# Order of a turn and of the feed-forward jobs in a six-layer attention stack on one core

## The chip, the cores and the metric

One core of a Trainium2 chip runs the whole program. The metric is device time in microseconds of one execution; the median of three runs of the kernel before is 1388.38 us (1385.80 to 1391.52). The engines are TensorE (PE, matrix products), VectorE (DVE), ScalarE (ACT), GpSimd (POOL) and SyncE (SP), which issues the transfers. Each works through its own list in order, and they meet only at semaphores. Banks are the eight PSUM banks of 128 x 512 fp32.

## The reference

Three blocks follow each other on x of 2 x 512 x 128, each with a residual and a layer norm: a Mamba block with a mixture of experts, a cross attention, and a stack of six layers. The change touches only the stack:

```python
def local_attention(q, k, v):      # windows of 32, each sees itself and the one before
    ...
    sim = jnp.einsum('bhwie,bhwje->bhwij', bq, bk2) * QK_SCALE
    sim = jnp.where(mask, -jnp.finfo(sim.dtype).max, sim)
    attn = jax.nn.softmax(sim, -1)
    out = jnp.einsum('bhwij,bhwje->bhwie', attn, bv2)
def attn_layer(x, Wqkv, qs, ksc, Wo):
    ...                            # 16 heads of 64: q, k = l2norm * scale, then rotary with a scale
def ffn_layer(x, g, bln, W1, b1, W2, b2):
    mu = x.mean(-1, keepdims=True)
    var = ((x - mu) ** 2).mean(-1, keepdims=True)
    xn = (x - mu) / jnp.sqrt(var + 1e-05) * g + bln
    hg = xn @ W1 + b1
    a, gate = jnp.split(hg, 2, -1)
    return a * jax.nn.gelu(gate, approximate=False) @ W2 + b2
for i in range(DEPTH):             # DEPTH = 6
    x = attn_layer(shift_tokens(x), ...) + x
    x = ffn_layer(shift_tokens(x), ...) + x
```

The hidden width of the feed-forward is 341, so gates and values come in groups of 128, 128 and 85 rows.

## The kernel before

The stack (`build_stack`) is a software pipeline of turns, 16 to a layer. Channels lie on the partitions and the 512 positions of a batch entry on the free axis. A layer has 16 units, eight for each of two batch entries; a unit h is q (even h) or k (odd h) of four heads on the side of projection and rotation, and a unit n is two heads on the side of scores, softmax and values. The first and the last layer stand alone; the four layers between run in a loop (`all_turns`, lines 1175 to 1180), so the first has four turns of filling before it and the last four turns of draining behind it.

In turn t the engines work on several units at once:

- PE (`body`, line 1370): scores of unit t+1 (line 1299 adds the mask, 1305 the products), projection of unit t+4 into two banks (1266 to 1270), transposes of the probabilities of unit t (1317), output projection of t-1 (1339), values' projection of t+1 (1290), head norm of t+4 (1278), values of t (1329).
- ACT (`body`, 1462): copy of the output of t-1 (1437), square of the projected pair (1413), exponential of the scores of t+1 (1481), copies of the transposed probabilities (1444) and of v (1453), logarithm and root for the head norm (1420, 1424).
- DVE (`body`, 1587): normalisation of unit t+3 (1543), in some turns a cast of the next layer's weights (1523), maximum (1603) and subtraction (1609) of t+1, the two rotary products of t+4 (1532, 1533), row sum (1626) and reciprocal (1630) of t+1.
- POOL (`body`, 1650): probabilities of unit t times the reciprocal (1657), sum of the two squares of t+4 (1666), the two sums of the rotary products of t+4 (1668, 1669), in some turns the low part of the next layer's weights (1648).
- SP (`body`, 1215): places the normalised heads of t+3 by transfers, four for q (1203) and eight for k (1207), then shifts v of t+1 (1212, 1213), then weights.

The two banks of the projected pair exist once: the projection of the next unit waits for both products of this one. The scores of an even unit need the k unit normalised one turn earlier. In turns 7 to 14 of all layers but the last, DVE and POOL also split the next layer's weights into a high and a low part (`high_weights`, `low_weights`), and in turns 11 and 12 ACT scales the rotary table (`scale_table`, 1431).

The feed-forward of a batch entry is a job of four stages, one in each of four turns (`Steps.stage`, 1169): t modulo 8 is 0 to 3. Job 0 of a layer lies in its turns 8 to 11, job 1 in turns 0 to 3 of the next layer. Stage 0: residual (1551), mean (1343), centring (1567), square (1501). Stage 1: variance at the head of PE's turn (1347), its root on ACT (1471, 1473), scale and shift (1574, 1576), gate 0 (1356) and value 0 (1363), gelu 0 (1459) and gate 1. Stage 2: gelu 1, value 1, gate 2, gelu 2, value 2. Stage 3: down projection (1368), second residual (1558), and the new stream split into a high part by ACT (1505) and a low part by DVE (1635), for which the projection of the first unit of that batch entry in the next layer waits. Gates are put into the job's output bank, values into the bank of v, so gates and values alternate one by one; each gelu has a table load before it and another behind it (1460), which brings back the table of logarithm and exponential.

Of the kernel before, what the change touches and what calls it, by code (L numbers as in the profile page):

```python
# [11 lines left out]
ALU = mybir.AluOpType  # L12
# [1073 lines left out]
def build_stack(nc, ctx, Y, places, spare, d, C):  # L1086
# [164 lines left out]
    def _(pe):  # L1251
# [28 lines left out]
        def project_v(s, n, before):  # L1280
# [4 lines left out]
            if before[1] in (1, 2):  # L1285
                pe.wait_ge(*act_done.at(s.turn, 3 * before[0] + (1 if before[1] == 1 else 3)))
# [62 lines left out]
        def up_gate(s, job, j):  # L1349

            if j == 0:
                pe.wait_ge(*ffn_in.at(s.turn, 80 * (job + 1) if job < 1 else 80))
                pe.wait_ge(*centre_step.at(s.turn, 3 * job + 3))
            else:
                pe.wait_ge(*gate_done.at(s.turn, 3 * job + j))
            mm(OUT_BANK[job % 2][0:ROWS[j], :], w1[:, HID + P * j:HID + P * j + ROWS[j]], xn[:], start=True, stop=True).then_inc(up_done.sem, 1)

        def up_value(s, t, job, j):

            pe.wait_ge(*v_copied.at(s.turn, min(t + 2, UNITS) if s.last else t + 2))  # L1360
            if act_done.any(s.turn, 3 * job + j):
                pe.wait_ge(*act_done.at(s.turn, 3 * job + j))
            mm(V_BANK[0:ROWS[j], :], w1[:, P * j:P * j + ROWS[j]], xn[:], start=True, stop=True).then_inc(up_done.sem, 1)
# [6 lines left out]
        def body(s):  # L1370
            for t in s.range:
                (job, stage), before = s.stage(t), s.stage(t - 1)
# [33 lines left out]
    def _(ac):  # L1406
# [48 lines left out]
        def gelu(s, job, j):  # L1455
            ac.wait_ge(*up_done.at(s.turn, 6 * job + (1, 3, 4)[j]))
            if act_done.any(s.turn, 3 * job + j // 2):
                ac.wait_ge(*act_done.at(s.turn, 3 * job + j // 2))
            A(gate[0:ROWS[j], j % 2, :], OUT_BANK[job % 2][0:ROWS[j], :], ACT.Gelu, bias=ffn_param[0:ROWS[j], 5 + j:6 + j]).then_inc(gate_done.sem, 1)
            nc.scalar.preload_act_table_set("natural_log_exp_and_others")  # L1460

        def body(s):
            for t in s.range:
                job, stage = s.stage(t)
                if t >= 0 and s.unit(t - 1):
                    copy_out(s, t - 1)
# [7 lines left out]
                if stage == 2:  # L1474
                    gelu(s, job, 1)
# [10 lines left out]
                if stage == 1:  # L1486
                    ac.wait_ge(*ffn_in.at(s.turn, 80 * (job + 1) if job < 1 else 80))
                    gelu(s, job, 0)
                if stage == 2:
                    gelu(s, job, 2)  # L1490
                if t in (11, 12) and not s.last:
                    ac.wait_ge(*product_done.at(s.turn, 2 * (t + 4)))
                    scale_table(s, t - 11, 1)
                if s.unit(t + 4):
                    logarithm(s, t + 4)
                    root(s, t + 4)
                if stage == 0:
# [3 lines left out]
                    A(dsq[:], dx[:], ACT.Square).then_inc(rstd_step.sem, 1)  # L1501
                if s.resplit(job, stage):
# [14 lines left out]
    def _(dv):  # L1517
# [60 lines left out]
        def gated(s, job, j):  # L1578
            rows = ROWS[j]
            dv.wait_ge(*gate_done.at(s.turn, 3 * job + j + 1))  # L1580
            dv.wait_ge(*up_done.at(s.turn, 6 * job + (2, 5, 6)[j]))
# [321 lines left out]
```

## Time and profile before

| | us |
|---|---|
| median of 3 runs | 1388.38 |
| the profiled execution, its own time | 1386.02 |
| its span | 1383.9 |
| PE busy | 1169.6 (85%) |
| DVE busy | 981.7 (71%) |
| ACT busy | 866.7 (63%) |
| POOL busy | 677.9 (49%) |

All times in the rows are microseconds from the start of the span. The stack runs from about 380 to 1371; a layer is about 155 to 161 us. Busy shares are those of the whole span, in which the stack is 70%; the order inside one turn has to be read from the timelines. The lines of the helper functions are those of the kernel before, and tiles of earlier blocks reused by the stack carry their old names (h is the squares, x the sine products, mo_w the cosine products or the normalised probabilities).

### The profile page before, as it was taken

To read this page: it belongs to the slowest core of one execution; us is meant where nothing else is said; L and a number is where in the kernel's file an instruction comes from. 1 tells how busy PE (TensorE), PEld (TensorE's weight loads), DVE (VectorE), ACT (ScalarE), POOL (GpSimd) and SP (SyncE) were. 2 spreads that over 40 slices of the span, in tenths; PEclk is the share of its full clock that TensorE was granted. 3 is DMA by queue.
4 is the path that set the end of the run, shared out by engine and by line. 5 is a ranking of instruction groups with operands and counts; after the bars stand their busy time and mean duration, and the time that the engine had idled before them with its cause. 6 is when DMAs were issued, how large, how long until landed. Compare 5 with 4: busy or idle time off the path is not lost. (4 is left out here: it accounts for less than half of the span.)

```text
span 1383.9 us, 27095 instructions
## 1 busy us (share of the span) xinstructions
PE 1169.6 (85%) x9636; PEld 720.0 (52%) x9636; DVE 981.7 (71%) x1207; ACT 866.7 (63%) x1284; POOL 677.9 (49%) x522
## 2 busy tenths in 40 slices
PE   7787789997658988998978988898988989899875
PEld 3222257774225555565555655565555555556541
DVE  2798867775647777867776787677876777777743
ACT  5553366664345677676867667586866758686744
POOL 1555434442246555646564565546564465645420
PEclk9899979999869999999999999999999999999997
DMA  3000053102013533434333433334333442434220
GB/s 104 1 0 0 1 129 122 55 1 70 23 31 91 144 76 86 110 101 104 77 99 83 127 82 86 101 87 122 78 91 86 113 106 71 103 84 113 68 60 15
DMA packets 75528, 107.32 MB, mean 78 GB/s; under 512 B 25347, under 2 KB 31938, under 8 KB 75002
## 3 DMA queue, kind: packets, MB, share of 16 engines
q1 hardware_dynamic: 75386, 105.47, 29.1%
q8 instruction: 84, 1.38, 0.4%
q14 instruction: 58, 0.48, 0.1%
HBM read 30.89 MB, written 0.59 MB: 23 GB/s over the span
## 5 line engine op out<-in xcount | busy, mean ns | idle before, releaser
L1543 DVE SCALAR_TENSOR_TENSOR st_turned<-st_rn,mo_w 128x1024 f32<-128x1024 f32 x96 | 154.9, 1613 | 150.6 <-POOL mo_w L1669 94.1
L1666 POOL TENSOR_TENSOR st_sq_sum<-h 128x512 f32<-128x512 f32 x96 | 126.6, 1318 | 220.6 <-ACT h L1413 220.6
L1668 POOL TENSOR_TENSOR mo_w<-mo_w,x 128x512 f32<-128x512 f32 x96 | 122.3, 1274 | 185.0 <-DVE mo_w L1533 185.0
L1413 ACT ACTIVATE h<-banks 128x1024 f32<-128x1024 f32 x96 | 98.3, 1024 | 145.8 <-PE banks L1270 145.7
L1532 DVE TENSOR_TENSOR x<-banks,st_scaled 128x1024 f32<-128x1024 f32 x96 | 116.8, 1217 | 26.2 <-ACT h L1413 25.9
L1329 PEld LDWEIGHTS banks<-st_p_blocks,st_vs 128*64 128x64 f32 x1536 | 83.0, 140 | 97.3 <-issue 96.0
L1278 PE MATMUL banks<-st_sq_sum,head_ones 128*128 128x512 f32 x192 | 105.8, 633 | 31.4 <-POOL st_sq_sum L1666 29.9
L1657 POOL TENSOR_TENSOR mo_w<-st_prob,st_ri 128x512 f32<-128x512 f32 x96 | 123.8, 1289 | 15.1 <-DVE st_ri L1630 14.5
L1290 PEld LDWEIGHTS banks<-st_wv,stream 128*128 128x128 f32 x768 | 100.7, 191 | 45.1 <-issue 45.0
L1329 PE MATMUL banks<-st_p_blocks,st_vs 128*64 128x64 f32 x1536 | 101.9, 231 | 25.1 <-ACT st_p_blocks L1444 24.9
L1669 POOL TENSOR_TENSOR mo_w<-mo_w,x 128x512 f32<-128x512 f32 x96 | 122.5, 1276 | 0.0
L1533 DVE TENSOR_TENSOR mo_w<-banks,st_scaled 128x1024 f32<-128x1024 f32 x96 | 116.5, 1214 | 0.0
L1444 ACT ACTIVATE st_p_blocks<-banks 64x512 f32<-64x512 f32 x192 | 112.1, 584 | 3.2 <-PE banks L1317 0.8
L430 POOL TENSOR_TENSOR ma_dbx<-ma_u,ma_b_rows 128x1024 f32<-128x1024 f32 x32 | 75.4, 2359 | 74.6 <-ACT ma_b_rows L288 51.6
L1481 ACT ACTIVATE st_prob<-st_prob 128x512 f32<-128x512 f32 x96 | 60.4, 629 | 77.4 <-DVE st_prob L1609 77.1
L1305 PE MATMUL banks<-st_k_blocks,st_qT 128*32 128x128 f32 x3072 | 108.7, 284 | 0.0
L1266 PE MATMUL banks<-st_y_high,st_w_high 128*128 128x512 f32 x192 | 90.6, 472 | 15.9 <-POOL st_w_low L1648 8.6
L1290 PE MATMUL banks<-st_wv,stream 128*128 128x128 f32 x768 | 101.2, 275 | 0.0
L1305 PEld LDWEIGHTS banks<-st_k_blocks,st_qT 128*32 128x32 f32 x3072 | 81.4, 113 | 37.6 <-issue 37.1
L1339 PE MATMUL banks<-x,st_wo 128*128 128x512 f32 x192 | 98.4, 594 | 0.8 <-ACT x L1437 0.8
L1329 PE MATMUL banks<-st_p_blocks,st_vn 128*64 128x64 f32 x1536 | 98.3, 225 | 0.0
L370 DVE TENSOR_TENSOR_SCAN ma_state<-banks,ma_dbx 128x512 f32<-128x512 f32 x64 | 76.0, 1213 | 13.5 <-ACT banks L298 11.0
(229 smaller groups left out, 2680.7 us busy)
## 6 DMA issues: line engine op xcount, KB each, us to landing
st_qT<-st_turned SPq DMA_DIRECT2D x192, 128.0 KB, 2.3
st_k_blocks<-st_turned SPq DMA_DIRECT2D x384, 64.0 KB, 2.0
st_vs<-st_vn SPq DMA_DIRECT2D x96, 192.0 KB, 2.5
st_w_raw<-in_w_qk SPq DMA_DIRECT2D x12, 512.0 KB, 5.3
st_vs<-st_vn SPq DMA_DIRECT2D x96, 48.0 KB, 2.1
mo_w_all<-gate_rows SPq DMA_DIRECT2D x1, 3072.0 KB, 13.0
st_wv<-in_w_v SPq DMA_DIRECT2D x12, 256.0 KB, 2.9
st_wo<-in_wo SPq DMA_DIRECT2D x12, 256.0 KB, 3.7
```

What stands on the lines that cost most here:

```text
L1278: mm(NORM_BANK, C["head_ones"], sq_sum[:], start=True, stop=True).then_inc(norm_done.sem, 1)
L1290: last = mm(V_BANK[:, rows], Y[:, b, rows], wv[:, pair, :], start=True, stop=True)
L1305: last = mm(SCORE_BANK[rows].rearrange("p (o h i k) -> p o h i k", o=2, h=2, i=2)[:, odd, :, i, :], qT[:, r, pair, t0:t0 + WIN], k_blocks[ ...
L1329: last = mm(TURN_BANK[rows, P * j:P * j + P].rearrange("p (h o q) -> p h o q", h=2, q=WIN)[:, :, odd, :], (vn if odd else vs)[:, r, j, row ...
L1444: A(p_blocks[rows, r, half, :], TURN_BANK[rows, :], ACT.Copy).then_inc(pt_copied.sem, 1)
L1532: v.tensor_tensor(sin_part[:], QK_BANKS, scaled[:, which, 1], ALU.mult).then_inc(product_done.sem, 1)
L1533: v.tensor_tensor(cos_part[:, which], QK_BANKS, scaled[:, which, 0], ALU.mult).then_inc(product_done.sem, 1)
L1543: v.scalar_tensor_tensor(turned[:, h % 4], rn[:, h % 2, :].unsqueeze(1).to_broadcast([P, 2, SEQ]), 1e12, cos_part[:, which], ALU.min, ALU. ...
L1657: nc.gpsimd.tensor_tensor(pn[:, r], prob[:, r], ri[:, r, :].unsqueeze(2).to_broadcast([P, 8, 64]), ALU.mult).then_inc(pn_done.sem, 1)
L1666: nc.gpsimd.tensor_tensor(sq_sum[:], sq[:, 0, :], sq[:, 1, :], ALU.add).then_inc(sq_summed.sem, 1)
L1668: nc.gpsimd.tensor_tensor(cos_part[:, which, 0, :], cos_part[:, which, 0, :], sin_part[:, 1, :], ALU.subtract).then_inc(add_done.sem, 1)
L1669: nc.gpsimd.tensor_tensor(cos_part[:, which, 1, :], cos_part[:, which, 1, :], sin_part[:, 0, :], ALU.add).then_inc(add_done.sem, 1)
```

## The change

No matrix product is added or taken away in number, and no transfer. The order of instructions on four engines changes, and what waits for what with it.

- DVE: in a turn the maximum and the difference come first, then normalisation, cast, and the feed-forward's residual, scaling or gating, then row sum and reciprocal; the rotary products come behind them, then centring or second residual.
- POOL: the sum of squares comes first, then the probabilities of unit t+1 (no longer of unit t, one turn later), then the two rotary sums.
- ACT: the copy of the output of unit t comes at the end of turn t, behind logarithm and root, no longer at the head of turn t+1; the gelus come behind it. Gelus 0 and 1 stand together in stage 1 with one restore of the table behind the pair. The scaling of the rotary table comes behind the copy of the output.
- PE: gate 1 goes to the bank of v at the end of stage 1, value 0 and value 1 come early in stage 2, value 2 early in stage 3, and the down projection in the same stage 3 behind the head norm. The output and values' projections keep their place before the head norm.

```diff
@@ PE, body
+                if stage == 2:
+                    up_value(s, t, job, 0)
+                    up_value(s, t, job, 1)
+                if stage == 3:
+                    up_value(s, t, job, 2)
                 if s.unit(t) and t >= 0:
                     turn_probs(s, t)
-                if stage == 3:
-                    down(s, job)
                 if t >= 0 and s.unit(t - 1):
                     out_proj(s, t - 1)
                 if t >= -1 and s.unit(t + 1):
-                    project_v(s, t + 1, before)
+                    project_v(s, t + 1, job, stage)
+                if s.unit(t + 4):
+                    head_norm(s, t + 4)
                 if stage == 0:
                     mean(s, job)
                 if stage in (1, 2):
-                    up_gate(s, job, 0 if stage == 1 else 2)
-                if s.unit(t + 4):
-                    head_norm(s, t + 4)
-                if stage in (1, 2):
-                    up_value(s, t, job, stage - 1)
+                    up_gate(s, t, job, 0 if stage == 1 else 2)
+                if stage == 3:
+                    down(s, job)
                 if s.unit(t) and t >= 0:
                     values(s, t)
                 if stage == 1:
-                    up_gate(s, job, 1)
-                if stage == 2:
-                    up_value(s, t, job, 2)
+                    up_gate(s, t, job, 1)
@@ ACT, gelu and body
-            ac.wait_ge(*up_done.at(s.turn, 6 * job + (1, 3, 4)[j]))
+            ac.wait_ge(*up_done.at(s.turn, 6 * job + (1, 2, 5)[j]))
-            A(gate[0:ROWS[j], j % 2, :], OUT_BANK[job % 2][0:ROWS[j], :], ACT.Gelu, ...)
-            nc.scalar.preload_act_table_set("natural_log_exp_and_others")
+            A(gate[0:ROWS[j], j % 2, :], (V_BANK if j == 1 else OUT_BANK[job % 2])[0:ROWS[j], :], ACT.Gelu, ...)
-                if t >= 0 and s.unit(t - 1):
-                    copy_out(s, t - 1)
...
-                if stage == 2:
-                    gelu(s, job, 1)
...
                 if s.unit(t + 4):
                     logarithm(s, t + 4)
                     root(s, t + 4)
+                if t >= 0 and s.unit(t):
+                    copy_out(s, t)
...
+                if stage == 1:
+                    ac.wait_ge(*ffn_in.at(s.turn, 80 * (job + 1) if job < 1 else 80))
+                    gelu(s, job, 0)
+                    gelu(s, job, 1)
+                    nc.scalar.preload_act_table_set("natural_log_exp_and_others")
+                if stage == 2:
+                    gelu(s, job, 2)
+                    nc.scalar.preload_act_table_set("natural_log_exp_and_others")
+                if t in (11, 12) and not s.last:
+                    ac.wait_ge(*product_done.at(s.turn, 2 * (t + 4)))
+                    scale_table(s, t - 11, 1)
@@ DVE, body: maximum and difference now stand ahead of this
+                if t >= -3 and s.unit(t + 3):
+                    normalise_heads(s, t + 3)
+                ...                                    # casts, as before
                 if stage == 0:
                     residual1(s, job)
                 if stage == 1:
                     scale_centred(s, job)
-                if s.unit(t + 4):
-                    rotate(s, t + 4)
-                if stage == 0:
-                    centre(s, job)
+                if stage == 2:
+                    gated(s, job, 0)
+                    gated(s, job, 1)
                 if stage == 3:
-                    residual2(s, job)
-                if stage == 2:
-                    gated(s, job, 1)
+                    gated(s, job, 2)
                 ...                                    # row sum and reciprocal of t + 1, as before
-                if stage in (1, 2):
-                    gated(s, job, 0 if stage == 1 else 2)
+                if s.unit(t + 4):
+                    rotate(s, t + 4)
+                if stage == 0:
+                    centre(s, job)
+                if stage == 3:
+                    residual2(s, job)
@@ POOL, body
-                ...                                    # probabilities of t, low weights, sum of squares, rotary sums
+                ...                                    # low weights, sum of squares
+                n = t + 1
+                if s.unit(n) and n >= 0:
+                    r = n % 2
+                    pool.wait_ge(*rec_done.at(s.turn, n + 1))
+                    if t_done.any(s.turn, n - 1):
+                        pool.wait_ge(*t_done.at(s.turn, n - 1))
+                    nc.gpsimd.tensor_tensor(pn[:, r], prob[:, r], ri[:, r, :]..., ALU.mult).then_inc(pn_done.sem, 1)
+                ...                                    # rotary sums of t + 4
```

## Rows read from the trace of the kernel before

**Rows 1.** The page's group of line 1543 (busy, mean ns, idle before, releaser).

```profile
L1543 DVE SCALAR_TENSOR_TENSOR st_turned<-st_rn,mo_w 128x1024 f32<-128x1024 f32 x96 | 154.9, 1613 | 150.6 <-POOL mo_w L1669 94.1
```

**Rows 2.** Timeline of DVE, one plain turn (start, us, engine, line, what, idle before).

```profile
781.37 0.68 DVE L1603 TENSOR_REDUCE st_mx<-banks 128x8 f32<-128x512 f32 x1
...
783.82 1.21 DVE L1533 TENSOR_TENSOR mo_w<-banks,st_scaled 128x1024 f32<-128x1024 f32 x1
...
785.66 0.20 DVE L1630 RECIPROCAL st_ri<-st_rs 128x8 f32<-128x8 f32 x1
787.65 2.05 DVE L1543 SCALAR_TENSOR_TENSOR st_turned<-st_rn,mo_w 128x1024 f32<-128x1024 f32 x1 [1.79 <-POOL mo_w L1669]
789.63 0.68 DVE L1603 TENSOR_REDUCE st_mx<-banks 128x8 f32<-128x512 f32 x1
```

**Rows 3.** Timeline of POOL, the same turn.

```profile
785.11 1.27 POOL L1668 TENSOR_TENSOR mo_w<-mo_w,x 128x512 f32<-128x512 f32 x1 [1.72 <-DVE mo_w L1533]
...
787.58 1.04 POOL L1657 TENSOR_TENSOR mo_w<-st_prob,st_ri 128x512 f32<-128x512 f32 x1
789.88 1.27 POOL L1666 TENSOR_TENSOR st_sq_sum<-h 128x512 f32<-128x512 f32 x1 [1.26 <-ACT h L1413]
```

**Rows 4.** Timeline of DVE, a normalisation with POOL idle.

```profile
750.50 1.22 DVE L1543 SCALAR_TENSOR_TENSOR st_turned<-st_rn,mo_w 128x1024 f32<-128x1024 f32 x1 [1.89 <-ACT st_rn L1424]
```

**Rows 5.** Timeline of PE, a stage 3 turn in which it never waits.

```profile
760.59 0.38 PE L1299 MATMUL banks<-mask,ident 128*128 128x512 bf16 x1
...
761.90 0.50 PE L1266 MATMUL banks<-st_y_high,st_w_high 128*128 128x512 f32 x1
...
763.84 2.74 PE L1368 MATMUL banks<-st_act,st_w 128*128 128x512 f32 x6
766.42 1.02 PE L1339 MATMUL banks<-x,st_wo 128*128 128x512 f32 x2
...
768.17 1.02 PE L1278 MATMUL banks<-st_sq_sum,head_ones 128*128 128x512 f32 x2
...
770.21 0.39 PE L1299 MATMUL banks<-mask,ident 128*128 128x512 bf16 x1
```

**Rows 6.** Timeline of ACT, the square of the same turn.

```profile
763.60 1.02 ACT L1413 ACTIVATE h<-banks 128x1024 f32<-128x1024 f32 x1 [0.89 <-PE banks L1270]
```

**Rows 7.** Timelines of SP and PE, where scores wait for k.

```profile
790.38 4.99 SPq L1207 DMA_DIRECT2D st_k_blocks<-st_turned  x8
...
794.27 0.39 PE L1299 MATMUL banks<-mask,ident 128*128 128x512 bf16 x1 [0.18 <-DMA st_k_blocks<-st_turned]
```

**Rows 8.** Source view of line 1523, ns min/median/max.

```profile
L1523 DVE CAST st_w_high<-st_w_raw x48: 280/708/1356, 388.3 to 1190.2; 128x256 fp32r<-128x256 f32 x48
```

**Rows 9.** Timeline of DVE, maxima of turns 0, 4, 8, 12, 15 of layer 1.

```profile
571.24 0.68 DVE L1603 TENSOR_REDUCE st_mx<-banks 128x8 f32<-128x512 f32 x1
...
612.87 0.69 DVE L1603 TENSOR_REDUCE st_mx<-banks 128x8 f32<-128x512 f32 x1
...
646.87 0.68 DVE L1603 TENSOR_REDUCE st_mx<-banks 128x8 f32<-128x512 f32 x1
...
690.72 0.69 DVE L1603 TENSOR_REDUCE st_mx<-banks 128x8 f32<-128x512 f32 x1
...
717.93 0.68 DVE L1603 TENSOR_REDUCE st_mx<-banks 128x8 f32<-128x512 f32 x1
```

**Rows 10.** Timelines of DVE and ACT, a stage 0.

```profile
1208.88 1.41 DVE L1551 TENSOR_TENSOR stream<-banks,stream 64x512 f32<-64x512 f32 x2
...
1213.72 0.61 ACT L1501 ACTIVATE st_dsq<-st_dx 128x512 f32<-128x512 f32 x1
```

**Rows 11.** Timeline of ACT, a table load in the drain.

```profile
1356.67 1.28 ACT L1459 ACT_TABLE_LOAD   x1 [3.62 <-PE banks L1356]
```

**Rows 12.** Timeline of PE and windows (us, engines' busy time, PEclk, DMA).

```profile
1185.61 0.48 PE L1329 MATMUL banks<-st_p_blocks,st_vs 128*64 128x64 f32 x4 [2.20 <-ACT st_p_blocks L1444]
...
1185.00:1188.50 3.50, 2.89 (x44) 2.34 (x47) 1.76 (x3) 2.96 (x5) 2.46 (x3) 0.57 0.24 70
```

More of the change, by code:

```diff
@@ L1278, in head_norm, with project_v @@
             mm(NORM_BANK, C["head_ones"], sq_sum[:], start=True, stop=True).then_inc(norm_done.sem, 1)
-        def project_v(s, n, before):
+        def project_v(s, n, job, stage):
             b, pair = n // 8 % 2, n % 8
@@ L1284, in project_v @@
                 pe.wait_ge(*v_copied.at(s.turn, n))
-            if before[1] in (1, 2):
-                pe.wait_ge(*act_done.at(s.turn, 3 * before[0] + (1 if before[1] == 1 else 3)))
+            if stage in (2, 3):
+                pe.wait_ge(*act_done.at(s.turn, 3 * job + stage))
             pe.wait_ge(*wv_in[pair // 4].at(s.turn, 16 * (n // 16) + 16))
@@ L1353, in up_gate, with up_value @@
                 pe.wait_ge(*centre_step.at(s.turn, 3 * job + 3))
-            else:
[L1355 to L1363, printed above, removed]
+            if j == 1:
+                pe.wait_ge(*v_copied.at(s.turn, min(t + 2, UNITS) if s.last else t + 2))
+            if j == 2:
+                pe.wait_ge(*act_done.at(s.turn, 3 * job + 1))
+            bank = V_BANK if j == 1 else OUT_BANK[job % 2]
+            mm(bank[0:ROWS[j], :], w1[:, HID + P * j:HID + P * j + ROWS[j]], xn[:], start=True, stop=True).then_inc(up_done.sem, 1)
+        def up_value(s, t, job, j):
+            if j < 2:
+                pe.wait_ge(*gate_done.at(s.turn, 3 * job + j + 1))
+            else:
+                pe.wait_ge(*v_copied.at(s.turn, min(t + 1, UNITS) if s.last else t + 1))
+                pe.wait_ge(*act_done.at(s.turn, 3 * job + 2))
+            bank = OUT_BANK[job % 2] if j == 0 else V_BANK
+            mm(bank[0:ROWS[j], :], w1[:, P * j:P * j + ROWS[j]], xn[:], start=True, stop=True).then_inc(up_done.sem, 1)
         def down(s, job):
@@ L1371, in body @@
             for t in s.range:
-                (job, stage), before = s.stage(t), s.stage(t - 1)
+                job, stage = s.stage(t)
                 if stage == 1:
@@ L1485, in body @@
                     copy_v(s, t + 1)
-                if stage == 1:
-                    ac.wait_ge(*ffn_in.at(s.turn, 80 * (job + 1) if job < 1 else 80))
-                    gelu(s, job, 0)
-                if stage == 2:
[L1490 to L1493, printed above, removed]
                 if s.unit(t + 4):
@@ L1589, in body @@
                 job, stage = s.stage(t)
-                if t >= -3 and s.unit(t + 3):
-                    normalise_heads(s, t + 3)
-                if s.first and t + 5 < PARTS:
-                    high_weights(s, t + 5, 0)
-                if t >= PARTS - 1 and t < 2 * PARTS - 1 and not s.last:
-                    high_weights(s, t - PARTS + 1, 1)
                 n = t + 1
@@ L1609, in body @@
                     v.tensor_tensor(prob[:, r], bank, mx[:, r, :].unsqueeze(2).to_broadcast([P, 8, 64]), ALU.subtract).then_inc(sub_done.sem, 1)
+                if t >= -3 and s.unit(t + 3):
+                    normalise_heads(s, t + 3)
+                if s.first and t + 5 < PARTS:
+                    high_weights(s, t + 5, 0)
+                if t >= PARTS - 1 and t < 2 * PARTS - 1 and not s.last:
+                    high_weights(s, t - PARTS + 1, 1)
                 if stage == 0:
@@ L1651, in body @@
             for t in s.range:
[L1652 to L1657 removed]
                 if s.first and t + 5 < PARTS:
                     low_weights(s, t + 5, 0)
[L1660 to L1662 removed]
+                h = t + 4
+                if s.unit(h):
                     pool.wait_ge(*sq_done.at(s.turn, h + 1))
```

21 lines of the change are left out of this document (7 added, 14 removed).

## The prediction

> **What bounds the kernel now.** I read the page's groups first. The stack's own groups occur 96 times each, one per turn, and the costliest VectorE group, the normalisation in line 1543, stands idle before its start for 150.6 us, 94.1 us of it for GpSimd's second sum (line 1669) [rows 1]. Then the timelines, engine by engine, over one undisturbed turn of the third layer. VectorE begins the maximum at 781.37 and the next one at 789.63: a turn is 8.26 us [rows 2]. The loop that sets this: the second product (line 1533) ends at 785.03; GpSimd starts the first sum 0.08 later and both take 2.47 up to the start of line 1657 [rows 2, 3]; the normalisation starts 0.07 after that (787.65), takes 2.05 and the maximum follows at once (789.63); from a maximum to the start of the second product are 2.45 (783.82 - 781.37), and that product takes 1.21 [rows 2]. 0.08 + 2.47 + 0.07 + 1.98 + 2.45 + 1.21 = 8.26, the whole turn. VectorE idles 1.79 in it. The normalisation's 2.05 is itself a price of the order: GpSimd's line 1657 runs beside it from 787.58 [rows 3], and where nothing runs beside it the same instruction takes 1.22 [rows 4].
>
> PE is the engine behind. A feed-forward turn in which it never waits shows all its steps: scores 1.31 (760.59 to 761.90), projection with transposes 1.94 (to 763.84), down projection 2.58 (to 766.42), output and value projections 1.75 (to 768.17), head norm and values 2.04 (to 770.21) [rows 5]. Without the down projection a turn costs PE 7.04. So a plain turn can lose at most 1.2 of its 8.26.
>
> **Plain turn, after.** Zero is the start of PE's scores. Projection starts at 1.31; ACT's square starts 1.70 after it (763.60 against 761.90) and takes 1.02 [rows 5, 6], so it ends at 4.03. GpSimd's sum of squares, now first on its queue, starts 0.08 later and takes 1.27 [rows 3]: 5.38. PE has by then done transposes, output and value projection (1.31 + 1.94 + 1.75 = 5.00) and waits 0.44 for it; head norm and values end at 5.44 + 2.04 = 7.48. On VectorE the maximum starts at 1.44, the subtraction ends at 2.84; the normalisation waits for the sums. They began after the products of the turn before, which end at 7.84: the exponential (square's end less the overlap, 3.93 + 0.63 = 4.56) releases the row sum; from a product's end to the reciprocal's start are 0.63, its length 0.20 (785.66) [rows 2], so reciprocal ends at 5.5, products at 7.84, sums at 7.92 + 2.47 = 10.4, which is 2.95 in a turn of 7.48. Normalisation alone then: 2.98 to 4.21, before the sum of squares starts at 4.11. Its old neighbour, line 1657, now runs beside the products. So VectorE and GpSimd no longer bound; 7.48 is PE's, with head norm's wait in it.
>
> But what is late next is the key transfer. After each odd unit SP issues eight transfers of k; the next scores need the first four. In the one place where PE is seen waiting for them, the first issue is at 790.38 and scores start at 794.27: 3.89 later [rows 7]. Before, normalisation ended at 789.70 and its late first issue left just enough. Now it ends at 4.21, so every second turn's scores come at 4.21 + 0.02 + 3.89 = 8.12 instead of 7.48. Mean of the pair: 7.80, against 8.26: a gain of 0.46 per plain turn. The shifts of v, queued on SP behind the eight issues (4.99 long), go out at 9.2 instead of on time; values wants them some 5 later, so that costs nothing.
>
> The eight turns a layer that also cast weights (line 1523) add 0.28 to 1.36, median 0.71 [rows 8]; it ran mostly beside line 1657 in its long form. Now it falls beside the sum of squares, so I take 1.1, nearer the long end. (The Trainium skill, GPSIMD Engine Reference, section Key points, says GpSimd contends with VectorE instructions of two SBUF inputs or in a two-port mode, the normalisation and the cast here; the 2.05 against 1.22 agrees. If the cast ran alone, some 0.8 per casting turn outside the feed-forward would go, 4 turns a layer.)
>
> **Feed-forward jobs.** Turn starts of layer 1 (the second) in VectorE's timeline give what they cost now [rows 9]: a job without casts 612.87 - 571.24 = 41.6; four turns after it 34.0; a job with casts 43.85; the next three 27.2 (with the fourth, as a plain turn of 8.3, 35.5).
> Stage 0, after: the residual (1.41 [rows 10]) now stands between normalisation and row sum; it also waits for the output projection, 3.25 + 1.02 + 0.04 = 4.31 [rows 5], so it ends at 5.72; row sum, reciprocal and products follow to 9.02; centring, of the maximum's size (0.68), 9.62; ACT's square 0.61 [rows 10], 10.27; variance, at the head of PE's next turn, from 10.3, one product of head norm's form, about 1.0, next scores 11.3. PE has been ready since 8.3 (7.48 and the mean's product). That is worse than now by 1.5, and it opens a gap of 2.0 on PE.
> Stage 1: scale and shift, two VectorE instructions of at most 0.7, end by 5.6, and gate 0 is wanted at 6.3; PE runs through with two more products of the output projection's form, half of that 1.75 each: 7.48 + 1.75 = 9.2. Stage 2: ACT does both gelus after one table load. A load is 1.28 [rows 11]; a gelu I take at 0.7, a little over the square of its size, 0.61 [rows 10]. Copy of the output ends at 9.0, so gelus end at 10.95 and 11.65, the restore at 12.9: in stage 2, 1.75, 2.4 and 3.7. Value 0 is wanted at 2.81: hidden. The square starts 0.7 late (3.7), sum of squares ends 6.1, head norm is wanted only at 6.8, after two value products: hidden too. PE: 7.04 + 3 x 0.88 = 9.7. One load and one restore less per job, 2.56 of ACT, lie under PE now and bring nothing in the middle of the stack. Stage 3: value 2, then everything, then down: square starts at 3.95 for the restore, head norm waits to 6.4, down and values end at 11.0.
> Sum without casts: 11.3 + 9.2 + 9.7 + 11.0 = 41.2, against 41.6.
> With casts: the turn before leaves the chain 1 us late and normalisation, cast and low part of the weights contend; stage 0 becomes 13.3 and PE's gap 2.5. At 1185.61 PE resumes after a gap of 2.20 and the granted clock of the next 3.5 us is 0.57, mostly the 1.2 GHz level [rows 12]. So I add 1.3 for half clock on variance, scores and projection: 13.3 + 1.3 + 9.2 + 9.7 + 11.0 = 44.5 against 43.85. (By the Trainium skill, TensorE: Matmul & The Clock Gate, section Part 1, a gap of this length would not lower the clock; the row says it can. By the page the sum would be 6.5 us lower over the five layers.)
> After a job: in the four turns without casts the low part of the stream makes normalisation end at 4.55 and the first scores come at 8.5, then 7.5, 8.1, 7.5: 31.6 against 34.0. After the job with casts ACT's table scaling (two instructions of the square's size, 2 us [rows 6]) now stands behind the copy of the output, which waits for values; the high part of the stream comes 2.2 late and the turn is 10.5; then 7.5, 8.9, 8.0: 34.9 against 35.5.
>
> **The sum.** Four turns after a job 2.4 x 5 = 12; first four turns of layer 0, 0.46 x 4 = 1.9; the last layer's four before the drain 1.8. Turns after the casting job 0.6 x 5 = 3. Casting jobs -0.65 x 5 = -3.3. Other full jobs 0.4 x 6 = 2.4. In the drain, with no other work, gelu 1 no longer waits for a restore and a load: 2.4, as PE waits for gelus there; the last turns without a projection 1. Sum 21.2, say 22 with the turns of the first filling. Against the profiled execution (span 1383.9, time 1386.0) that is 1364; the median of the runs shown is 2.4 above the profiled one, so **1366**. The stall where the layer loop jumps back is not touched by any of this and stays.
> Bounds of what no row prices: the key transfer's 3.89 was seen beside other loads; if scores can start at 7.48 every plain turn gives 0.32 more (9 us over 28). If it is 1 us longer, the pair is 16.6 and the plain gain is gone (13 us). The half clock: nothing to 1.7 per job, so -6.5 to +14 against the sum.
>
> **Rivals.** (a) More: keys land in time and the clock holds at full in stage 0. For it: row 794.27 had loads of weights queued ahead. Against: issue of transfers alone spaces the first four by 1.8. 1366 - 9 - 6.5 = 1350.
> (b) Nothing measurable: the variance at the head of the turn, with products ahead of centring, costs each of the 12 jobs 1.5 us more than I have, because PE's gap grows over 2 us in all of them and each is followed by half clock: 1366 + 12 x 1.5 = 1384. For it: gaps of 2.0 and 2.5 against the 2.2 that is seen to drop. Against: gaps of 1.5 to 1.6 are many and harmless.
> (c) Slower: the key transfer sets every turn pair. The point from which it decides is normalisation ending at 5.0 in the even turn, where the pair is 8.9 + 7.5, today's. If normalisation meets the sum of squares and takes its 2.05, it ends at 5.1 and delays head norm by 0.8 as well: 9.0 + 8.3 = 17.3, 0.4 a turn more than now over 28 turns, 11, and the jobs lose 1 each: about 1398. Against: alone it ends just as the sum of squares starts.
>
> **Numbers.** Mine 0.55, (a) 0.22, (b) 0.13, (c) 0.10. What this measurement can tell from no change is about 0.5%, 7 us. Faster: mine and (a), a little of (b): 0.80; same 0.10; slower 0.10. Range 1342 to 1390: it takes in (a), (b) and the edge of (c).
>
> **What would show it.** Maximum to maximum in plain turns alternating near 7.5 and 8.1, with PE's scores released by the transfer of k in every second; normalisation at 1.2 in nearly all turns and line 1657 at 1.04; PE waiting about 0.4 for the sum of squares each turn; variance waiting 2 us and more behind ACT's square, with a lower granted clock after it; 24 table loads for gelu instead of 36. It is wrong if normalisation still takes 2 us, or stage 0 to stage 1 takes no more than 10 us.

## Result and the profile after

The changed kernel takes 1395.38 us (median of 20 runs, 1390.10 to 1405.55) against 1389.14 for the kernel before beside it (20 runs): ratio 1.0046, 95% interval 1.0029 to 1.0062. It is about 6 us slower, where 1366 was forecast and 1390 was the upper end of the range. The profiled execution has a span of 1393.5 us against 1383.9.

The page of the changed kernel: busy time, the maximum and the normalisation.

```profile
PE 1180.0 (85%) x9636; PEld 733.1 (53%) x9636; DVE 959.0 (69%) x1207; ACT 838.0 (60%) x1260; POOL 664.6 (48%) x522
...
L1604 DVE TENSOR_REDUCE st_mx<-banks 128x8 f32<-128x512 f32 x96 | 66.4, 692 | 199.5 <-PE banks L1305 199.2
...
L1550 DVE SCALAR_TENSOR_TENSOR st_turned<-st_rn,mo_w 128x1024 f32<-128x1024 f32 x96 | 124.9, 1302 | 9.7 <-POOL mo_w L1679 5.3
```

Line 1550 is the normalisation, 1543 before. Its idle time fell from 150.6 us [rows 1] to 9.7 and its mean from 1613 ns to 1302. DVE, ACT and POOL are all less busy, and the time is longer: what VectorE waits for now is the scores, 199.2 us before the maximum (10.8 before the change). So the wait named in the forecast went; the question is what PE's scores are late for.

Timeline of DVE, a plain turn of the changed kernel, the one that answers to [rows 2].

```profile
783.39 0.69 DVE L1604 TENSOR_REDUCE st_mx<-banks 128x8 f32<-128x512 f32 x1 [3.13 <-PE banks L1305]
784.11 0.69 DVE L1610 TENSOR_TENSOR st_prob<-banks,st_mx 128x512 f32<-128x512 f32 x1
784.72 1.22 DVE L1550 SCALAR_TENSOR_TENSOR st_turned<-st_rn,mo_w 128x1024 f32<-128x1024 f32 x1
786.52 0.69 DVE L1630 TENSOR_REDUCE st_rs<-st_prob 128x8 f32<-128x512 f32 x1 [0.58 <-ACT st_prob L1483]
787.24 0.20 DVE L1634 RECIPROCAL st_ri<-st_rs 128x8 f32<-128x8 f32 x1
787.43 1.23 DVE L1539 TENSOR_TENSOR x<-banks,st_scaled 128x1024 f32<-128x1024 f32 x1
788.58 1.21 DVE L1540 TENSOR_TENSOR mo_w<-banks,st_scaled 128x1024 f32<-128x1024 f32 x1
790.98 0.69 DVE L1604 TENSOR_REDUCE st_mx<-banks 128x8 f32<-128x512 f32 x1 [1.19 <-PE banks L1305]
```

This turn is 7.59 us where 7.48 was walked out, and the next is 8.07 where 8.12 was. The plain turn is what the prediction said. PE's timeline shows what it waits for. The rows are, in order of time: the variance of a casting job, the first projection behind it, the scores waiting for k (first behind a job, then in a later turn), and the variance of a job of layer 5.

```profile
654.76 2.08 PE L1347 MATMUL banks<-st_dsq,mean_ones 128*128 128x512 f32 x2 [2.39 <-ACT st_dsq L1497]
...
691.29 0.49 PE L1266 MATMUL banks<-st_y_high,st_w_high 128*128 128x512 f32 x1 [2.03 <-ACT st_y_high L1512]
...
781.92 0.39 PE L1299 MATMUL banks<-mask,ident 128*128 128x512 bf16 x1 [1.82 <-DMA st_k_blocks<-st_turned]
797.58 0.39 PE L1299 MATMUL banks<-mask,ident 128*128 128x512 bf16 x1 [0.42 <-DMA st_k_blocks<-st_turned]
...
1222.81 1.12 PE L1347 MATMUL banks<-st_dsq,mean_ones 128*128 128x512 f32 x2 [1.86 <-ACT st_dsq L1497]
```

Windows of the changed kernel behind three of these waits, and (from 853.10) behind the wait at the first projection one layer later, 2.03 us as well (us, busy time of PE, PEld, DVE, ACT, POOL, then granted clock, share and GB/s of DMA).

```profile
652.50:654.70 2.20, 0.00 (x0) 0.00 (x0) 1.54 (x2) 1.14 (x2) 1.17 (x1) 0.92 0.49 121
654.70:658.30 3.60, 3.54 (x35) 1.67 (x35) 0.00 (x0) 1.32 (x3) 1.99 (x3) 0.58 0.09 31
...
689.20:691.30 2.10, 0.07 (x5) 0.02 (x1) 0.11 (x1) 1.96 (x3) 0.00 (x0) 1.00 0.00 0
691.30:694.90 3.60, 3.60 (x11) 2.75 (x12) 3.30 (x5) 0.85 (x1) 0.00 (x0) 0.58 0.01 2
...
853.10:856.70 3.60, 3.50 (x17) 2.45 (x18) 3.53 (x5) 1.62 (x3) 0.52 (x1) 1.00 0.01 2
...
1221.00:1222.80 1.80, 0.00 (x0) 0.00 (x0) 1.09 (x2) 1.22 (x2) 1.23 (x2) 1.00 0.40 99
1222.80:1224.20 1.40, 1.39 (x7) 0.52 (x11) 0.00 (x0) 0.23 (x1) 1.26 (x2) 1.00 0.64 179
1224.20:1227.80 3.60, 3.60 (x37) 2.85 (x35) 1.92 (x3) 1.09 (x2) 0.00 (x0) 0.53 0.23 69
```

After three of these waits PE works some 3.6 us mostly at the 1.2 GHz level (a mean of 0.53 to 0.58 of 2.4 GHz). Behind the variance of layer 5, the shortest of them, the fall begins only 1.4 us later. After the fourth, as long as the second, the clock stays at 1.00.

Behind a job k comes later than the 3.89 us from first issue to scores that the prediction took from [rows 7]: 5.19 here (776.73 to 781.92) against 3.90 in the later turn (793.68 to 797.58). SP's timeline has the eight issues of each place, and the DMA view of the same stretches (776.7:782.9 and 793.7:798.7; transfers, MB, share) has on the first a packet of queue q8, which the profile calls instruction, and none on the second:

```profile
776.73 6.13 SPq L1207 DMA_DIRECT2D st_k_blocks<-st_turned  x8
q8 instruction: 1, 0.02, 1.5%
...
793.68 5.00 SPq L1207 DMA_DIRECT2D st_k_blocks<-st_turned  x8
q1 hardware_dynamic: 513, 0.44, 38.0%
```

This holds for the whole trace. Of the 48 places of k, 18 have an issue that took 0.80 to 1.89 us instead of 0.59, and each of these has such a packet (16 KB, 0.92 to 1.57 us long) in it. 24 have no packet of q8 and no slow issue. In the other six it lies at the edge, with the last issue or already running at the first. PE waits for k 23 times. In 13 of them the scores start 3.86 to 3.94 after the first issue. In nine they start 4.60 to 5.68 after it, eight of them in the first turn behind a job, and in all nine the packet starts 2.3 to 3.2 us after the first issue. The loads of weights don't go with it: in five of the turns with 3.9 the feed-forward's five loads stand directly ahead of k. No run moved the packets, so this is what the trace shows side by side, not a cause shown by an edit.

A table by stage, from the starts of the scores in PE's timelines (not of the maxima as in [rows 9]): us for four turns. "Stall" is the loop's jump between turns 15 and 0, which both kernels have three times.

```
                      before            after             walked out
turns 0 to 3 (job)    41.7 (layer 1)    42.1 (layer 1)    41.2
turns 4 to 7          32.1 to 32.3      32.7 to 33.0, and 31.6
 (layers 1 to 5)                        34.7 (layer 4)
turns 8 to 11 (casts) 43.6, and         44.5 to 45.0, and 44.5
                      44.5 (layer 0)    43.6 (layer 4)
turns 12 to 15        37.3, 37.4        36.0, 36.8        34.9
 (layers 0 and 4, no stall)
last layer's job 0    42.5              43.1              41.2
```

### The profile page after: what moved, and what is told of

The parts are those of the page before. It is cut to its first block and busy times, and to the rows that moved or that the text cites. A ratio compares the mean times of both kernels' runs of the same rounds, so it can differ in the third digit from the quotient of the medians.

```text
span 1393.5 us, 27040 instructions
## 1 busy us (share of the span) xinstructions
PE 1180.0 (85%) x9636; PEld 733.1 (53%) x9636; DVE 959.0 (69%) x1207; ACT 838.0 (60%) x1260; POOL 664.6 (48%) x522
## 5 line engine op out<-in xcount | busy, mean ns | idle before, releaser
L1667 POOL TENSOR_TENSOR st_sq_sum<-h 128x512 f32<-128x512 f32 x96 | 133.2, 1387 | 247.5 <-ACT h L1420 247.5
L1604 DVE TENSOR_REDUCE st_mx<-banks 128x8 f32<-128x512 f32 x96 | 66.4, 692 | 199.5 <-PE banks L1305 199.2
L1674 POOL TENSOR_TENSOR mo_w<-st_prob,st_ri 128x512 f32<-128x512 f32 x96 | 100.1, 1042 | 71.7 <-DVE st_ri L1634 71.7
L1550 DVE SCALAR_TENSOR_TENSOR st_turned<-st_rn,mo_w 128x1024 f32<-128x1024 f32 x96 | 124.9, 1302 | 9.7 <-POOL mo_w L1679 5.3
L1329 PEld LDWEIGHTS banks<-st_p_blocks,st_vs 128*64 128x64 f32 x1536 | 78.3, 138 | 74.0 <-issue 72.6
L1305 PE MATMUL banks<-st_k_blocks,st_qT 128*32 128x128 f32 x3072 | 112.2, 290 | 0.0
L1427 ACT ACTIVATE st_rn<-banks,fill 128x512 f32<-128x512 f32 x96 | 66.0, 687 | 57.5 <-PE banks L1278 57.5
## 6 DMA issues: line engine op xcount, KB each, us to landing
mo_w_all<-gate_rows SPq DMA_DIRECT2D x1, 3072.0 KB, 12.8
```

The lines of the kernel that those rows point to most:

```text
L1305: last = mm(SCORE_BANK[rows].rearrange("p (o h i k) -> p o h i k", o=2, h=2, i=2)[:, odd, :, i, :], qT[:, r, pair, t0:t0 + WIN], k_blocks[ ...
L1329: last = mm(TURN_BANK[rows, P * j:P * j + P].rearrange("p (h o q) -> p h o q", h=2, q=WIN)[:, :, odd, :], (vn if odd else vs)[:, r, j, row ...
L1550: v.scalar_tensor_tensor(turned[:, h % 4], rn[:, h % 2, :].unsqueeze(1).to_broadcast([P, 2, SEQ]), 1e12, cos_part[:, which], ALU.min, ALU. ...
L1667: nc.gpsimd.tensor_tensor(sq_sum[:], sq[:, 0, :], sq[:, 1, :], ALU.add).then_inc(sq_summed.sem, 1)
```

## Experiments

All ratios are of medians to the kernel before on the same chip, with 95% intervals; the changed kernel stands at 1.0046.

**Fill the gap before the variance.** The idle stretch is filled with work that changes nothing.

```diff
                 if stage == 1:
+                    pe.wait_ge(*sub_done.at(...))
+                    for i in range(8):
+                        mm(SCORE_BANK, C["ident16"], C["mask16"], start=True, stop=True, ...)
                     variance(s, job)
```

> The changed kernel with eight bf16 products of mask and identity (512 columns, overwritten afterwards by the scores) ahead of the variance in each of the 12 jobs; results are unchanged. In the trace of the changed kernel PE waits 1.76 to 2.39 us there for ACT's square and then runs some 3.5 us at a granted clock near 0.53. Theory A (the half clock behind the gap is what the sum missed): the gap is filled, the clock stays at 1.00 in the stretch behind it, stage 1 goes from about 10.9 to 9.6 us, and the time falls by 8 to 17 us, to 1380 to 1388. Rival B (the gap itself costs, the clock does not, since PE has slack behind): the clock rises but the time stays within 4 us of 1395. Rival C (the fillers end later than the square and push the variance back): slower than 1396.

Measured: 1387.43 us, 0.9967 (0.9947 to 0.9987): 0.8% or 11 us less than the changed kernel, with more work in it. PE's timeline and windows of this kernel at the casting job of layer 1 (of the eight fillers the trace has seven):

```profile
657.86 1.67 PE L1385 MATMUL banks<-mask,ident 128*128 128x512 bf16 x7 [0.16 <-issue]
660.09 1.13 PE L1347 MATMUL banks<-st_dsq,mean_ones 128*128 128x512 f32 x2 [0.56 <-ACT st_dsq L1503]
```

```profile
658.00:659.80 1.80, 1.53 (x7) 0.48 (x5) 1.38 (x2) 0.73 (x2) 0.94 (x1) 1.00 0.25 58
659.80:663.40 3.60, 3.31 (x39) 2.07 (x40) 0.85 (x2) 1.56 (x3) 2.24 (x3) 1.00 0.27 77
```

The variance comes no earlier, but what follows runs at full clock, in all 12 jobs: stage 1 of a casting job takes 9.9 us instead of up to 11.0. In the two profiled executions the jobs differ by 6.8 us, which is the part of the 11 that the traces place. Theory A holds, B falls. In one point A was too broad: in the jobs of layers 1 to 4 without casts, stage 1 took 9.8 in both kernels; PE's gap was 1.75 to 1.77 there and the rate held. The clock fell in four of the five casting jobs (all with gaps of 2.39; in layer 4's it stayed at 1.00), to between 0.58 and 0.69, and in the two jobs of layer 5 that stand among full turns (1.86 and 1.87), to 0.53 and 0.60.

**Late variance.** The variance goes behind the projection, its root behind the exponential, scale and shift behind the reciprocal.

```diff
-                if stage == 1:
-                    variance(s, job)
                 if t >= -1 and s.unit(t + 1):
                     scores(s, t + 1)
                 if s.unit(t + 4):
                     project(s, t + 4)
+                if stage == 1:
+                    variance(s, job)
...
                     v.reciprocal(...)
+                if stage == 1:
+                    scale_centred(s, job)
```

> The changed kernel with the variance behind the projection on PE, its root behind the exponential on ACT, scale and shift behind the reciprocal on DVE. Theory A (the centring chain at the head of PE's turn costs each job its gap of about 2 us and the half clock of about 1.4 us): 12 x 2.5 to 3.4 us less, 1355 to 1368. Rival B (only moved: gate 0 then waits for scale and shift, and the products end later, so the gap reappears in front of gate 0 or of the next projection): 1385 to 1395, with PE waiting 1.5 us or more at gate 0.

Measured: 1380.51 us, 0.9919 (0.9901 to 0.9938), 1.3% or 18 us under the changed kernel: between A and B. The wait at the head of the turn is gone, and a part is given back at gate 0, as this row of PE shows.

```profile
663.40 1.13 PE L1359 MATMUL banks<-st_xn,st_w 128*128 128x512 f32 x2 [1.78 <-DVE st_xn L1583]
```

The first turn of a casting job fell from 12.8 or more to 9.4, the next rose from between 9.9 and 11.0 to between 12.7 and 14.3; cast, normalisation and row sum now stand before the scaling on DVE. These second turns also price the half clock by itself. All five have the wait at gate 0 (1.70 or 1.78); in two the clock stays at 1.00 and the turn is 12.7, in three it falls and the turn is 14.1 to 14.3. One window of each kind:

```profile
663.40:667.00 3.60, 3.45 (x44) 1.90 (x49) 2.21 (x2) 1.32 (x2) 1.31 (x2) 1.00 0.17 48
983.10:986.70 3.60, 3.51 (x34) 2.00 (x34) 2.30 (x3) 0.00 (x0) 1.22 (x1) 0.54 0.17 51
```

**Table scaling behind the high part.** ACT splits the stream first and scales the rotary table after.

```diff
-                if t in (11, 12) and not s.last:
-                    ...scale_table(s, t - 11, 1)
                 if s.resplit(job, stage):
                     ...A(y_high[:, job % 2, :], Y[:, job % 2, 0:SEQ], ACT.Copy)...
+                if t in (11, 12) and not s.last:
+                    ...scale_table(s, t - 11, 1)
```

> The changed kernel with ACT's scaling of the rotary table behind the high part of the stream instead of ahead of it, in turns 11 and 12. In the changed kernel's trace PE waits 2.03 us at the first projection behind each of the five jobs with casts. Theory A (the wait and the half clock behind it are on the path): the wait goes, turn 12 goes from 11.6 to about 9, and the time falls by 7 to 14 us against the changed kernel (1.0046 of before), to 0.995 to 1.000. Rival B (the chain is as late by the second residual and the low part): at most 3 us less.

Measured: 1379.87 us, 0.9921 (0.9894 to 0.9947), 1.2% or 17 us under the changed kernel. ACT's timelines, first of the changed kernel, then of this one:

```profile
687.97 0.60 ACT L1444 ACTIVATE x<-banks 128x512 f32<-128x512 f32 x1 [2.23 <-PE banks L1329]
688.46 2.18 ACT L1438 ACTIVATE st_scaled<-st_table,st_rope_scale 128x1024 f32<-128x1024 f32 x2
690.54 0.62 ACT L1512 ACTIVATE st_y_high<-stream 128x512 fp32r<-128x512 f32 x1
```

```profile
688.09 0.60 ACT L1444 ACTIVATE x<-banks 128x512 f32<-128x512 f32 x1 [2.23 <-PE banks L1329]
688.59 0.62 ACT L1509 ACTIVATE st_y_high<-stream 128x512 fp32r<-128x512 f32 x1
689.11 2.18 ACT L1438 ACTIVATE st_scaled<-st_table,st_rope_scale 128x1024 f32<-128x1024 f32 x2
```

Turn 12 falls from between 10.9 and 12.3 us to between 9.4 and 10.0, and PE waits at the projection no more. Rival B falls. Theory A holds in its cause, and the gain is above its 7 to 14 us. The profiled executions place 10 of the 17 us in turns 12 to 15.

**q and k change places, and then the weights move too.** k goes to the even units and q to the odd ones (columns of the weights, scales and rotary tables laid out so), and in the second kernel the feed-forward's weights are also loaded one turn earlier.

```diff
-                    if which == 0:
+                    if which == 1:
                         src, dst = 64 * pair, 64 * part
@@ second kernel only, SP
-                if t == 5:
+                if t == 4:
                     ...load_ffn(turn)
```

> The changed kernel with the order of the units turned round: k in even units, q in odd ones (weights, scales and rotary tables laid out accordingly), so that the scores of an even unit wait for the first two of four transfers of q instead of the first four of eight of k. Theory K (the key transfer sets the start of the scores: 23 waits, 22.8 us in PE's timeline of the changed kernel): the waits go, and the time falls by 12 to 23 us, to 1372 to 1383. Rival L (the waits lie beside others: DVE's or POOL's chain is as late): at most 4 us less, 1391 to 1396, with the same distances between scores and another releaser.

> The kernel with k in even and q in odd units (1.0063 of before), and the feed-forward's weights loaded in turn 4 instead of 5, so that they are issued behind a place of q and not between a place of k and one of q. Theory K (SP's list of issues in order is what delays the heads: eight of k, two shifts and five weight loads ahead of q cost turns 6 and 7 of each layer about 2 and 1.5 us in x4_swap): both turns return to 8.1 and 7.6, the time falls by 10 to 20 us to 0.990 to 0.998. Rival L (heads late are covered by other chains): within 4 us of x4_swap.

Measured: the swap alone 1401.17 us, 1.0063 (1.0036 to 1.0089): no gain, theory K missed as written. With the weights moved 1378.41 us, 0.9918 (0.9892 to 0.9944), 1.4% under the swap alone. SP's timeline of the swap alone, in layer 2, tells why:

```profile
791.20 5.75 SPq L1207 DMA_DIRECT2D st_k_blocks<-st_turned  x8
796.99 0.59 SPq L1212 DMA_DIRECT2D st_vs<-st_vn  x1
797.64 0.58 SPq L1213 DMA_DIRECT2D st_vs<-st_vn  x1
798.43 0.42 SPq L1187 DMA_DIRECT2D st_w<-in_w  x1
799.14 1.34 SPq L1189 DMA_DIRECT2D st_w<-in_w  x3
800.66 0.36 SPq L1190 DMA_DIRECT2D st_ffn_param<-in_ffn_param  x1
801.21 2.44 SPq L1203 DMA_DIRECT2D st_qT<-st_turned  x4
```

Ten microseconds of issues follow without a break, and q, for which the scores now wait, is last. In layers 1 to 4 the turn behind a job fell from between 9.2 and 10.0 us to 7.9, and turns 6 and 7 rose by more, from about 8.1 and 7.6 to 9.6 or more and 9.2. PE waits for q nine times, 18.5 us. Once the loads are out of the way it waits twice, 5.7 us, and turns 4 to 7 of layers 1 to 5 take 30.7 us, where the changed kernel took 32.7 or more. So in these layers it is the place in SP's list of issues that made q late. In layer 0 it is the landing. There q goes out directly behind three loads of the next layer's weights and scales, the second transfer, the last that the scores need, lands 6.7 us after its issue, PE waits 4.69 us and the turn is 12.4 us, which takes back some 5 us of the gain:

```profile
454.33 1.07 SPq L1059 DMA_DIRECT2D st_w_raw<-in_w_qk  x2
455.44 1.11 SPq L1070 DMA_DIRECT2D st_rope_scale<-in_rope_scale  x1
456.65 2.44 SPq L1203 DMA_DIRECT2D st_qT<-st_turned  x4
...
463.96 0.39 PE L1299 MATMUL banks<-mask,ident 128*128 128x512 bf16 x1 [4.69 <-DMA st_qT<-st_turned]
```

**The same two edits on the kernel before.**

> The kernel before with the two edits to the transfers alone: k in even and q in odd units, feed-forward weights in turn 4. If late heads are a cost that only the changed order has (PE of the kernel before waits for transfers 4 times, 1.3 us in all), the time stays within 0.4% of before: 1385 to 1396. If the transfers bound the kernel before too, behind other waits, it falls by 8 us or more, to 1382 or less.

Measured: 1388.10 us, 0.9985 (0.9968 to 1.0003). No gain beyond 0.3%: late heads are a cost that only the changed order has.

**The order of the turn without the two gate groups.** The kernel before, with the new order on DVE, POOL and ACT's copy; gates and values one by one.

```diff
@@ DVE, body of the kernel before
+                ...maximum and difference, then normalise_heads, casts, residual1 or scale_centred
                     v.reciprocal(...)
+                if s.unit(t + 4):
+                    rotate(s, t + 4)
+                ...centre, residual2, gated 1, then gated 0 or 2
```

> The kernel before with the order inside the turn alone changed: on DVE maximum and difference first and rotary products behind the reciprocal, on POOL sum of squares first and probabilities of t+1, on ACT copy of the output at the end of the turn; the feed-forward's gates and values stay one by one as before (gate 1 and value 1 on DVE behind the products). Theory A (plain turns gain about 0.5 us each, and the loss is the centring chain, which this order has too): between 1385 and 1397, within 0.5% of the changed kernel. Rival D (the two gate groups per job are what loses): clearly under 1380. Rival E (the two gate groups gain, and hide a loss of the order): over 1400.

Measured: 1406.95 us, 1.0108 (1.0081 to 1.0134), 0.6% slower than the changed kernel. It is over 1400, as rival E has it: the order of the turn is the half of the change that loses (about 15 us), and what this kernel leaves out is the half that gains (about 9). That half is more than the two gate groups: the order of head norm, mean, gates and down projection on PE and the later scaling of the rotary table belong to it, and no run takes them apart. Its two variances of layer 1 wait 1.65 and 1.22 us, and gate 0 another 1.1 for scale and shift, so this kernel has the centring chain too.

**All together.** Late variance, gate 0 behind the values, table behind the high part, k in even units, weights in turn 4.

```diff
-                if stage in (1, 2):
-                    up_gate(s, t, job, 0 if stage == 1 else 2)
+                if stage == 2:
+                    up_gate(s, t, job, 2)
                 ...values(s, t)
                 if stage == 1:
+                    up_gate(s, t, job, 0)
                     up_gate(s, t, job, 1)
```

> All together: variance behind the projection, root behind the exponential, scale behind the reciprocal, gate 0 behind the values, table scaling behind the high part, k in even units, feed-forward weights in turn 4. If the costs named (centring chain, table scaling, transfer issue) are separate, the gains add: 0.9919 for the variance, about 0.993 for the table, about 0.993 for the transfers against the changed kernel: 0.975 to 0.985 of before, 1356 to 1370. If they cover each other, 0.988 to 0.992 as the variance alone.

Measured: 1348.60 us, 0.9704 (0.9678 to 0.9729): 3.0% faster than the kernel before and 3.4% than the changed one, and more than the 0.975 to 0.985 expected, which had counted 0.7% each for table and transfers. Measured alone, variance, table and transfers gave 1.2 to 1.3% each against the changed kernel; their product would be 0.967 of before. So the gains add within the intervals. The place of gate 0 behind the values, which no other run has, shows no gain of its own. PE's timeline of the casting job in layer 1:

```profile
651.93 0.50 PE L1266 MATMUL banks<-st_y_high,st_w_high 128*128 128x512 f32 x1
...
653.42 1.02 PE L1347 MATMUL banks<-st_dsq,mean_ones 128*128 128x512 f32 x2
...
657.30 1.13 PE L1278 MATMUL banks<-st_sq_sum,head_ones 128*128 128x512 f32 x2 [0.67 <-POOL st_sq_sum L1668]
...
660.21 1.98 PE L1359 MATMUL banks<-st_xn,st_w 128*128 128x512 f32 x4 [0.70 <-DVE st_xn L1584]
...
662.03 0.38 PE L1299 MATMUL banks<-mask,ident 128*128 128x512 bf16 x1
```

No wait in these rows reaches 1 us; the longest of the job is 1.47, ahead of the values' projection at 669.49, and the granted clock of the whole job (641.00:686.00) is 1.00. Layers 2 and 3 are 152.7 and 152.8 us with their stall (layer 2: 40.7, 30.7, 43.3 and 38.0) against 160.0 and 160.5 before.

## Why the prediction was wrong

*What held.* The walk of the plain turn: 7.59 and 8.07 measured, 7.48 and 8.12 walked; normalisation at 1.22 (median 1.216) and the probabilities' product at 1.04 in all 96; the new wait for k, with 3.86 to 3.94 us from first issue to scores in 13 of 23 places; stage 2 (9.6 against 9.7) and casting jobs as a whole (43.6 to 45.0 against 44.5); 24 table loads for gelu instead of 36; a gain in the drain (3.3 against 2.4). Neither of the two signs that were to show the forecast wrong came, and it was wrong all the same: both looked at VectorE and at the variance, and the loss lay elsewhere.

*What failed* is the walk of the turns behind a job. Two of its terms were too low: the key transfer's 3.89, which was taken for every place (4.60 to 5.68 measured in nine), and turn 12 with its "10.5" (10.9 to 12.3 measured). And the gain of 2.4 in each four turns behind a job was counted from VectorE's starts, where PE had 1.0 to give. By the parts of the table and the profiled executions, the change is 31.6 us worse than the sum (9.6 slower instead of 22 faster). The parts, each measured less walked out, over all its turns:

- Turns 12 to 15, five layers: 10.7 us. The prediction has "the high part of the stream comes 2.2 late and the turn is 10.5". The lateness was right (a wait of 2.00 to 2.03 in all five), the turn is 10.9 to 12.3. The clock fell behind that wait in layers 1 and 4 alone (10.9 and 12.3 us); in layers 0, 2 and 3 it stayed at 1.00 and the turn is 11.6 to 11.9, because the next scores wait 1.57 to 1.93 for k (layer 4 has both, its wait being 1.28). The prediction had charged half clock only behind the variance, and no late k. The edit that takes the wait at the projection away is worth 17 us.
- Turns 4 to 7, and 0 to 7 of layer 0: 10.6. "The key transfer's 3.89" was 4.6 to 5.7 in nine of the 23 places where PE waits for k, mostly the first turn behind a job; they are the ones with a packet of q8 early among the issues. Over 3.89 these nine make some 10 us, about half of it here and half in turns 12 to 15. Behind two of them the clock fell as well, and a turn of 7.6 us became 9.1. This is the bound "if it is 1 us longer" of the prediction, true in nine places instead of all. The 23 waits make 22.8 us. The 3.89 was read in "the one place where PE is seen waiting"; the kernel before has four such places, and behind its jobs, at 773.08 and 1094.13, scores start 4.91 after the first issue.
- Jobs without casts: 6.5. Stage 1 took 9.8 where 9.2 was walked, and 11.0 and 10.6 in the two of layer 5 where the clock fell. What was charged for clock in casting jobs, 6.5 us, was somewhat too high: filling the gap took 4.4 us out of them.
- The last layer's turns without a projection: 3.3, a transfer wait of 2.03 among them. The start of the stack: 2.1, which lies before the first instruction of the change and is no effect of it.
- Casting jobs, and the drain: -0.2 and -0.9. (10.7 + 10.6 + 6.5 + 3.3 + 2.1 - 1.1 is 32.1; the half microsecond left over is not placed.)

The trace agrees in part with rival (b), PE's gaps growing with half clock behind some of them. It agrees with rival (c) in that the transfer of k comes late, but not in its cause: the normalisation of 2.05 that (c) needs did not come, 80 of 96 took 1.22. Neither had its full price.

There is also a wrong reading under the forecast. [Rows 9] are starts of VectorE's maximum, and give 34.0 us for the turns behind a job; the scores of the same turns start within 32.3. VectorE comes out of a job late and PE is then ahead; turn 4 took PE 7.6 to 7.8 us before the change, not 8.26. The steady turn of [rows 2] is reached only after two or three undisturbed turns, and a layer has four at a time. A gain of 2.4 in each of these stretches was counted; PE's own count shows a loss of 0.4 to 0.7, and of 2.4 in layer 4. The sum over a layer does not change with the engine, but the room for a gain does: PE had only 1.0 us a stretch to give above 7.8 a turn.

*What the experiments show and what they don't.* Shown, each by an edit: the half clock behind the variance's gap (11 us), the place of the variance with it (18), the table ahead of the high part (17), SP's order of issue (20, on the kernel with k and q changed over), and that the edits to the transfers gain nothing in the old order. Not shown apart: the clock's share in the 17 of the table, and whether the packets of q8 make k late or only fall together with it, since no kernel moved them; nor did one try the loads alone at another place with q and k as they were.

## What to carry to other kernels

A steady turn read from one engine is not yet a price: read the length of the same stretch on the engine that the gain would have to go through, and over the turns that come after a disturbance. When an order is tightened, walk every list in order past the point of the gain, SP's issues too; here two steps that had been free in the slack, a table scaling and five weight loads, became the next bound. Moving the first was worth 17 us and moving the second, with q and k changed over, 18, where the change had lost 6. A landing time read in one place is a row too: read it in all places before it is multiplied by the turns. And a gap on PE can cost twice, once as itself and again as the half clock behind it: in the late-variance kernel three of five equal gaps of about 1.7 us did, at 1.5 us each. So the longer gaps are to be removed before smaller, more frequent ones.

## What the runs showed of the hardware

- The length of a gap on PE does not decide by itself whether the granted clock falls behind it. Among full turns it stayed at 1.00 behind every gap of 1.41 to 1.61 us in the kernels before and after. Behind 1.70 to 2.39 both occur: it fell, to between 0.53 and 0.69 over 3.6 us, behind 1.70 and 1.78 (late variance), 1.86, 1.93, 2.03 and 2.39 (changed kernel), and it stayed at 1.00 behind 1.78 (late variance), 1.75 to 1.82, 2.03 twice and 2.39 once (changed kernel) and 2.39 twice (table kernel). With the gap filled by bf16 products it stayed at 1.00 in all 12 jobs. The Trainium skill, TensorE: Matmul & The Clock Gate, section Part 1, gives a longer idle stretch than these as what lowers it; the measurement decides here.
- SP issues a transfer of 64 KB about every 0.62 us: eight take 4.96 to 5.01 us when nothing comes between. With a 16 KB packet of q8 (the queue that the profile calls instruction) among them one of the issues took 0.80 to 1.89 us, the eight up to 6.26, and where it came 2.3 to 3.2 us after the first issue the fourth transfer landed up to 1.8 us later.
- The profiled start of the stack differed by up to 6 us between kernels that are identical up to it (389.5 to 395.6), so single executions are to be compared from the first instruction that differs.
